# A decoder layer with 160 experts: a shared expert worked off at the end, and routing reordered

## The reference

```python
x = layernorm(x + self_attention(x))             # 16 heads of 16
x = layernorm(x + cross_attention(x, ctx_1024))  # similarity attention over the context
x = layernorm(x + experts(x))

# cross_attention: 16 sequences of 128, w1, w2, w3 = thirds of w_sim
Sim   = (hc @ w1)[:, :, None] + (hq @ w2)[:, None, :] + einsum('bid,bjd->bij', hc * w3, hq) + b
A     = softmax(Sim, axis=2)
hq_hat = A @ hq
Batt  = softmax(max(Sim, axis=2), axis=1)
hc_bar = sum_i Batt_i * hc_i
out   = concat([hc, hq_hat, hc * hq_hat, hc * hc_bar]) @ W_qv + b_qv

# experts: 160 of them, 8 for each token
probs = sigmoid(x @ router_w.T + expert_bias)
top_w, top_idx = top_k(probs, 8); top_w = 2.5 * top_w / sum(top_w)
routed = sum over the 8 of weight * (silu(x @ w_gate[e].T) @ w_down[e].T)
shared = silu(x @ w_gate_shared.T) @ w_down_shared.T
out = routed + shared
```

## Time and profile before

| | us | share of the span |
|---|---|---|
| median of 3 runs | 1225.49 | |
| the profiled execution | 1215.55 | |
| its span | 1213.7 | |
| TensorE matmul busy | 884.6 | 73% |
| TensorE weight load busy | 584.8 | 48% |
| VectorE busy | 542.4 | 45% |
| ScalarE busy | 437.9 | 36% |
| GpSimd busy | 394.1 | 32% |

### The profile page before, as it was taken

How to read it: one execution, slowest core, us unless ns; L and a number is a source line. 1 busy time by engine, 2 the same in 40 slices (tenths; PEclk the granted TensorE clock), 3 DMA queues, 4 the chain that set the end, 5 groups by cost and what they waited for, 6 DMA issues and landing times. The chain is left out here.

```text
span 1213.7 us, 17246 instructions
## 1 busy us (share of the span) xinstructions
PE 884.6 (73%) x4098; PEld 584.8 (48%) x4098; DVE 542.4 (45%) x1287; ACT 437.9 (36%) x942; POOL 394.1 (32%) x398
## 2 busy tenths in 40 slices
PE   8989999996697958677100578777787877786291
PEld 4433333432474735445100467666666656665271
DVE  1867777771327636465360122222232222222087
ACT  3257767775315142241000233333343433343011
POOL 7000000000000162543737255555555555555000
PEclk9979999998799978878655688898897888988596
DMA  7999999985101132221315677777777787774492
GB/s 251 296 371 334 326 365 360 347 307 174 45 35 53 50 111 97 76 84 53 126 67 206 213 229 241 232 227 222 232 235 244 220 235 224 227 232 114 188 420 82
DMA packets 113323, 247.22 MB, mean 204 GB/s; under 512 B 29378, under 2 KB 49770, under 8 KB 107008
## 3 DMA queue, kind: packets, MB, share of 16 engines
q1 hardware_dynamic: 92928, 209.39, 53.0%
q0 software_dynamic: 18240, 35.22, 8.0%
q10 hardware_dynamic: 2112, 2.10, 0.5%
HBM read 137.12 MB, written 125.70 MB: 217 GB/s over the span
## 5 line engine op out<-in xcount | busy, mean ns | idle before, releaser
L1517 POOL DMA_INDIRECT contributions<-e_y,e_dest x252 | 245.1, 973 | 227.5 <-ACT e_y L1504 158.6
L1483 DVE COPY e_xt<-e_psx 128x256 f32<-128x256 f32 (+1 forms) x196 | 97.1, 499 | 304.1 <-PE e_psx L1426 184.5
L1437 PE MATMUL e_psg<-e_xt,e_w 128*128 128x128 f32 (+1 forms) x784 | 173.7, 350 | 70.4 <-issue 35.9
L1648 POOL DMA_INDIRECT row_pool<-rows,places x128 | 125.6, 981 | 243.0 <-issue 159.1
L1446 PE MATMUL e_psy<-e_w,e_g 128*128 128x256 f32 x504 | 163.5, 429 | 40.9 <-ACT e_g L1497 21.1
L1437 PEld LDWEIGHTS e_psg<-e_xt,e_w 128*128 128x128 f32 x784 | 130.5, 219 | 86.9 <-issue 43.0
L493 DVE TENSOR_REDUCE a_mx<-a_psS 128x2 f32<-128x1024 f32 x128 | 152.2, 1218 | 35.5 <-PE a_psS L316 35.4
L451 ACT ACTIVATE a_e<-a_psT 128x512 f32<-128x512 f32 x256 | 137.8, 596 | 60.7 <-PE a_psT L346 52.8
L1504 ACT ACTIVATE e_y<-e_psy,e_weight 128x256 f32<-128x256 f32 x252 | 113.2, 473 | 98.7 <-PE e_psy L1446 55.6
L1497 ACT ACTIVATE e_g<-e_psg 128x128 f32<-128x128 f32 (+1 forms) x196 | 60.3, 308 | 197.6 <-PE e_psg L1437 119.6
L1426 PE MATMUL e_psx<-c_ident,e_x 128*128 128x128 f32 x504 | 96.1, 294 | 45.0 <-DMA e_x<-row_pool 44.9
(11 more groups left out here) (220 smaller groups left out, 981.1 us busy)
## 6 DMA issues: line engine op xcount, KB each, us to landing
row_pool<-fill SPq DMA_DIRECT2D x32, 1820.0 KB, 10.9
e_w<-w SPq DMA_DIRECT2D x196, 256.0 KB
e_x<-row_pool SPq DMA_DIRECT2D x140, 140.0 KB
c_c<-contributions SPq DMA_DIRECT2D x16, 1024.0 KB, 13.7
e_x<-row_pool SPq DMA_DIRECT2D x56, 280.0 KB
a_k<-k_parts SPq DMA_DIRECT2D x64, 128.0 KB, 5.8
a_q<-q_parts SPq DMA_DIRECT2D x32, 128.0 KB, 7.2
a_q<-q_parts SPq DMA_DIRECT2D x64, 64.0 KB, 6.9
```

The source lines that it names most:

```text
L1437: last = nc.tensor.matmul(psG[:, f.k % 2, 0:n], W[:, f.slot, c * INTER:(c + 1) * INTER], XT[:, f.k % 2, c * n:(c + 1) * n], start=c == 0, ...
L1483: nc.vector.tensor_copy(XT[:, at.k % 2, 0:n], psX[:, at.k % 2, 0:n]).then_inc(xt_done, 1)
L1517: nc.gpsimd.indirect_dma_start(out=contrib, out_offset=bass.IndirectOffsetOnAxis(ap=dest[:, page(f) + k:page(f) + k + 1], axis=0), in_=Y[: ...
L1648: nc.gpsimd.indirect_dma_start(out=pool, out_offset=bass.IndirectOffsetOnAxis(ap=place[:, b % 2, t, k:k + 1], axis=0), in_=rows[:, b % 2, ...
```

## The change

- The four similarities of a step go to banks 4, 5, 2 and 3 (`SIMILAR`), and none of them waits for an exponent. `rank` uses banks 0 to 2 and now waits for the third exponent.
- The numbers of the chosen experts come from an index search (`max_index`) in the choice, one for each tile, with a conversion of the result and the weights' product. `pack` and `unpack` are gone, with their buffers.
- `grow` moves from behind the products to ahead of the attention sums, `places` and the signal `rows_done` from behind the products to ahead of them.
- The shared expert leaves the steps. The last step has it for all four batches: gates 0 and 1 ahead of `rank`, gates 2 and 3 behind, four sigmoids on ScalarE, then, behind the tables, four gate multiplications, four products and four sums. The four results have buffers that the stage no longer needs by then, and SP stores all four behind its loads of the weights.
- Batch 2's scatters are in three groups: tile 0; tile 1 behind the end of mixing of batch 3; tiles 2 and 3 behind the router's products of batch 3.
- `rows`, `places` and `x2t` have four buffers, one for each batch, and the normalization no longer waits for scatters two batches back.

How the instructions stand is shown for four places. In these rows a name without a prefix is a tile in SBUF or memory, `m_ps` is the PSUM of the stage, and "x4" means four alike in a row.

The diff, cut to its core (the bodies of the removed functions are in the listing above):

```diff
+SIMILAR = (4, 5, 2, 3)
+GATES = (3, 6, 7, 5)
+SHARES = (0, 2, 6, 0)
...
-        X1T, ET, HQ, PR, X2T = (sb(f"m_{n}", [P, DC, S]) for n in ("x1t", "et", "hq", "pr", "x2t"))
-        GS, XS = sb("m_gs", [P, S]), sb("m_xs", [P, TT, D])
+        X1T, ET, HQ, PR = (sb(f"m_{n}", [P, DC, S]) for n in ("x1t", "et", "hq", "pr"))
+        X2T = sb("m_x2t", [P, B, DC, S])
         A, AT = sb("m_a", [P, TT, S]), sb("m_at", [P, TT, S])
+        GS, XS = A, (O, X1, X1b, AT[:, 0:2].rearrange("p a (t d) -> p (a t) d", d=D))
...
+        names8 = sb("m_names8", [P, TT, TOP_K], U32)
...
+                sp.dma_start(x2d[b], XS[b][:]).then_inc(x2_stored, 16)
...
-                store(n)
...
-            store(B - 2)
-            store(B - 1)
...
+            for b in range(B):
+                store(b)
...
-                    dispatch(b, sent[b % 2], range(TT))
+                    dispatch(b, sent[b % 2], (0,))
+                    pool_eng.wait_ge(mixed, TT * B)
+                    dispatch(b, sent[b % 2], (1,))
+                    pool_eng.wait_ge(routed, B)
+                    dispatch(b, sent[b % 2], (2, 3))
...
-                pe.wait_ge(shared_added, m_done)
...
+            def gate(b):
+                for c in range(DC):
+                    last = nc.tensor.matmul(ps[:, GATES[b]], Ws[:, c * INTER:(c + 1) * INTER], X2T[:, b, c],
...
+                last.then_inc(shared_gated, 1)
...
+                pe.wait_ge(shared_silu, b + 1)
+                if b == 3:
+                    pe.wait_ge(shared_added, 1)
+                out = two(SHARES[b])
...
+                    last = nc.tensor.matmul(out[:, t], GS[:, b, t * P:(t + 1) * P], Ws[:, DC * INTER:], start=True, stop=True)
...
                 if not part_b:
-                    share(n)
+                    gate(0)
+                    gate(1)
                     rank(n)
+                    gate(2)
+                    pe.wait_ge(lg_done, B)
+                    gate(3)
                     pe.wait_ge(spread_done, 1)
                     for i in range(3):
                         last = nc.tensor.matmul(ps[:, 4, i * P:(i + 1) * P], ones32[:], spread[:, i], start=True, stop=True)
                     last.then_inc(tables_spread, 1)
+                    pe.wait_ge(ranks_read, B)
+                    for b in range(B):
+                        share(b)
...
                 def similarity(i):
-                    if i >= 2:
-                        pe.wait_ge(row_expd, tile(i - 2))
...
-                        last = nc.tensor.matmul(ps[:, 4 + i % 2], ET[:, c, i * P:(i + 1) * P], CT[:, c],
+                        last = nc.tensor.matmul(ps[:, SIMILAR[i]], ET[:, c, i * P:(i + 1) * P], CT[:, c],
...
-                if part_c:
-                    share(n)
...
                 if part_c:
+                    pe.wait_ge(row_expd, tile(TT - 2))
                     rank(n)
...
-                for c in range(DC):
...
+                        nc.scalar.activation(A[:, i], ps[:, SIMILAR[i]], ACT.Exp, bias=nmax[:, i:i + 1],
...
+                    for b in range(B):
+                        act.wait_ge(shared_gated, b + 1)
+                        nc.scalar.activation(GS[:, b], ps[:, GATES[b]], ACT.Sigmoid).then_inc(shared_sigmoid, 1)
...
-                if n >= 2:
-                    act.wait_ge(sent[n % 2], n // 2 * (16 * TT * TOP_K))
...
+                normalize(nc, rows[:, n, :, 0:D], two(4), y[:, TT:], shift[:, TT:], normed2)
...
-                def gate_shared():
...
+                    for t in range(TT):
+                        do(nc.vector.max_index(names8[:, t], top[:, t], pr[:, t]))
+                    o2.hold()
+                    do(nc.vector.tensor_scalar(rows[:, n - 1, :, NAMES:ROW].bitcast(I32), names8[:], -1.0, float(EXPERTS),
+                                               ALU.mult, ALU.add))
+                    do(nc.vector.tensor_tensor(rows[:, n - 1, :, D:CODES], top[:], repeated(winv[:], 2, TOP_K), ALU.mult))
+                    sync()
+                def gate_shared(b):
...
+                def add_shared(b):
...
-                def pack():
...
-                def unpack():
...
-                    do(nc.vector.tensor_scalar(place[:, u_], k8[:], -1.0, FAR, ALU.mult, ALU.add))
-                    do(nc.vector.tensor_copy(rows[:, u_, :, CODES:NAMES], slots[:]))
...
                     dve.wait_ge(similar, tile(i))
-                    nc.vector.tensor_reduce(nmax[:, i:i + 1], ps[:, 4 + i % 2], AX, ALU.max, negate=True).then_inc(row_maxed, 1)
...
-                if part_c:
-                    gate_shared()
...
-                if part_c:
-                    pack()
-                    add_shared()
...
                 if part_c:
                     count_rows()
-                if part_c and not part_b:
-                    unpack()
                 if part_b:
                     dve.wait_ge(g_spread, n + 1)
                     nc.vector.tensor_scalar(ng[:], ps[:, 4, P:P + 1], -1.0, None, ALU.mult).then_inc(ng_done, 1)
-                if part_c and part_b:
-                    unpack()
+                if part_c:
+                    grow()
+                if part_c and not part_b:
+                    places()
+                    dve.sem_inc(rows_done, 1)
...
+                if part_c and part_b:
+                    places()
+                    dve.sem_inc(rows_done, 1)
...
-                if part_c:
-                    grow()
-                    places()
-                    dve.sem_inc(rows_done, 1)
...
                     dve.sem_inc(tables_done, 1)
+                    for b in range(B):
+                        gate_shared(b)
+                    for b in range(B):
+                        add_shared(b)
...
+        rows = ctx.enter_context(nc.sbuf_tensor("rows", [P, B, TT, ROW], F32))
...
+        place = ctx.enter_context(nc.sbuf_tensor("places", [P, B, TT, TOP_K], U32))
```

More of the change, by code:

```diff
@@ L565, in normalize @@
                              bias=shift[:, i:i + 1]).then_inc(done, 1)
-CONSTS = {"ident": P, "below": P, "far": EXPERTS, "home": EXPERTS, "expert": EXPERTS, "field": EXPERTS, "entry": 3, "slot": TOP_K * TT}
+CONSTS = {"ident": P, "below": P, "far": EXPERTS, "home": EXPERTS, "expert": EXPERTS, "entry": 3, "slot": TOP_K * TT}
 COL = {}
@@ L798, in rank, with share @@
                 last.then_inc(ranked, 1)
-            def share(m_done):
-                pe.wait_ge(shared_silu, m_done)
-                out = two(0)
+            def gate(b):
+                for c in range(DC):
+                    last = nc.tensor.matmul(ps[:, GATES[b]], Ws[:, c * INTER:(c + 1) * INTER], X2T[:, b, c],
+                                            start=c == 0, stop=c == DC - 1)
+                last.then_inc(shared_gated, 1)
+            def share(b):
+                pe.wait_ge(shared_silu, b + 1)
+                if b == 3:
+                    pe.wait_ge(shared_added, 1)
+                out = two(SHARES[b])
                 for t in range(TT):
-                    last = nc.tensor.matmul(out[:, t], GS[:, t * P:(t + 1) * P], Ws[:, DC * INTER:], start=True, stop=True)
+                    last = nc.tensor.matmul(out[:, t], GS[:, b, t * P:(t + 1) * P], Ws[:, DC * INTER:], start=True, stop=True)
                 last.then_inc(shared_made, 1)
@@ L906, in step @@
                     project_heads(n + 1)
[L907 removed]
+                turn(rows[:, n], 6, x2_turned, normed2, n * TT)
                 pe.wait_ge(x2t_done, n + 1)
@@ L912, in step @@
                     for c in range(DC):
-                        last = nc.tensor.matmul(lgs[:, t, 0:EXPERTS], X2T[:, c, t * P:(t + 1) * P], Wr[:, c],
+                        last = nc.tensor.matmul(lgs[:, t, 0:EXPERTS], X2T[:, n, c, t * P:(t + 1) * P], Wr[:, c],
                                                 start=c == 0, stop=c == DC - 1)
@@ L917, in step @@
                     turn_x1(n + 1)
-                for c in range(DC):
-                    last = nc.tensor.matmul(ps[:, 6], Ws[:, c * INTER:(c + 1) * INTER], X2T[:, c],
-                                            start=c == 0, stop=c == DC - 1)
-                last.then_inc(shared_gated, 1)
             run(pe, start, step)
@@ L1083, in add_shared @@
+                def add_shared(b):
+                    dve.wait_ge(shared_made, b + 1)
+                    shared = two(SHARES[b])
                     for t in range(0, TT, 2):
[L1084 removed]
+                        last = nc.vector.tensor_tensor(XS[b][:, t:t + 2], shared[:, t:t + 2], rows[:, b, t:t + 2, 0:D], ALU.add)
                     last.then_inc(shared_added, 1)
[L1087 to L1098 removed]
@@ L1173, in places @@
                     o2.hold()
-                    do(nc.vector.tensor_scalar(place[:, u_], k8[:], -1.0, FAR, ALU.mult, ALU.add))
-                    do(nc.vector.tensor_copy(rows[:, u_, :, CODES:NAMES], slots[:]))
+                    do(nc.vector.tensor_scalar(place[:, n - 1], k8[:], -1.0, FAR, ALU.mult, ALU.add))
```

(1 more changed line is left out.)

61 lines of the change are left out of this document (7 added, 54 removed).

## The result

The changed kernel takes 1192.55 us (median of 4 runs, 1191.65 to 1195.01) beside 1225.52 us of the kernel before: ratio 0.9734, 95% interval 0.9716 to 0.9751. The forecast was 1191. Its profiled execution took 1192.81 us, span 1190.8. The size came out; the way to it was another in part.

A forecast was written before the change was run, and what follows sets the result against it. GpSimd's scatters were taken to bound the end of mixing: 34.7 us earlier less 1 gives 34, so 1215.55 profiled becomes 1181.6, plus 9.9 for timed runs, 1191 us. The range was 1168 to 1209.

The forecast's parts named there:

- The bound: End of mixing: GpSimd's queue is the bound; batch 3's last scatter starts at 629.9 instead of 664.56, 34.7 us earlier.
- the 1 us for scatters beside VectorE's work: Last 48 back-to-back scatter issues: some slowed beside counts, tables and shared expert, 1 us taken, between 0 and 7.
- rival B: Similarities of steps 2 and 3: their signals are not held, starts near 433 and 493; gain 54 us, 1171; chance 0.22.
- The reference time: Whole kernel: profiled execution goes from 1215.55 to 1181.6 us; 9.9 added for the median of timed runs, 1191.
- All of it lies under the scatters: hidden: Shared expert between 590 and 631: loads to 613, stores by 620, no cost; without that cover some 20 us.
- Rival D: End of mixing: table's signal held until batch 3's scatters are out, stores open the barrier at about 675; 1229; chance 0.06.
- Gone is one gate product, off the path: Each mixing step: one gate product of TensorE leaves, off the path, so no time was counted for it.
- The index search: Choice ahead of row maximum 2: costs 1.8 us; with packing and shared sum moved away, gains 2.2 us per step.
- The counts fill the idle stretch: VectorE ahead of the attention sums: 9.9 us of counts fill idle time; only step 3 runs about 0.9 us late.
- The wait costs nothing: Batch 2's last sixteen scatters wait for the router's products: no cost while batch 3's places are not ready.
- The hold: Mixing stage: TensorE's signals are seen late in long unbroken scatter runs, some 2.3 to 4 us behind the last issue.
- A: The forecast itself: similarities of steps 2 and 3 both held, row maxima near 448 and 518; gain 34 us; chance 0.50.

The follow-up runs named there:

- r1: The kernel before, unchanged, profiled again in another surrounding: 1049.24 us.
- r9: The changed kernel with an unread gate product of TensorE put back in steps 0 to 2: 1039.57 us, ratio 0.9944 to the kernel before.
- r5: The changed kernel, unchanged, run again in another surrounding: 1040.79 us beside 1045.69 of the kernel before, ratio 0.9964.
- r7: The kernel before with the index search in place of packing and unpacking, nothing else: 1037.47 us, ratio 0.9939 to the kernel before.
- r3: The changed kernel with growing, places and the rows' signal behind the products again: 1040.82 us, ratio 0.9931 to the kernel before.
- r4: The changed kernel with batch 2's 32 scatters in one run again: 1036.44 us, ratio 0.9899 to the kernel before.

## Why the prediction was right, and where it was wrong

- **The bound** was right: the end of the mixing stage follows batch 3's first scatter. It followed batch 2's last with 0.3 us of idle, as forecast. The four index searches took 0.32 us each, and the 1 us for scatters beside VectorE's work came to 1.4 (62.0 us from 560.57 to 622.55, for 47 steps of 1.29).
- **Two errors cancelled.** The last scatter was forecast for 629.9 and started at 622.55, 7.4 us better, because the similarities were not held (434 and 498, near rival B's 433 and 493): row maximum 1 of step 3 came at 503.8, not at 519.0. Of these 15 us the rest of the step, with its 3.88 us of held signal and the early growing, gave 6.6 back. The barrier came 9.8 us worse than the forecast's distance from the last scatter. 34 forecast, 32.2 measured at the barrier. That these met is luck, not method.
- **The reference time** was luck too. The sum gave 1181.6 us for a profiled execution, and that took 1192.81. The forecast added 9.9 us, because the profiled execution of before was so much faster than its timed runs; the profiled execution of after was not, and its part behind the barrier is 9.3 us longer. r1 was to tell why, and could not, since it ran elsewhere; it stays open.
- **"All of it lies under the scatters: hidden"** failed. The 14 loads were sized at 11.6 us; in that surrounding 13 of them took 38.86. The shared products were not thought of as held at all; two of their sums waited 18.38 and 16.23 us, and the last store went out behind the last sum. Both paths ended within about 1 us of each other. Rival D had the stores as the opener of the barrier, by held tables; the tables were in time (587), the queue behind them was slow.
- **"Gone is one gate product, off the path"** failed in the first step: with it goes what kept TensorE's clock up, and row maximum 1 comes 1.5 us (r9 against r5) to 2.5 us (r7 against r3) later. In the later steps the clock fell with the product as well.
- **The index search** was right in price, 1.7 us (forecast 1.8), but worth 5.4 us in the step from 375, not 2.2, and 0.3 and 0.8 in the next two, which began at the lower clock in r7 and at the higher in r1. In the first the packing had also left TensorE idle: from 383 to 400 us it was busy for 11.6 of 17 us in r1 and for 13.5 in r7, at a granted clock of 0.71 and 0.90.
- **"The counts fill the idle stretch"** failed: the stretch was 6.91 us with 3.4 of unpacking beside it, but the faster row path shortened it to 6.01, and growing takes 9.9. It costs 2.4 to 2.8 us a step (r5 against r3) and brings batch 2's rows forward all the same.
- **"The wait costs nothing"** failed: the queue was the bound, and it paused for 2.30 and 2.88 us. Batch 3's places were ready at 579.2 and its first scatter went out at 581.54, so by an estimate from these rows up to 2.3 us of it was lost in the first result; where nothing is held it is some 3 to 4 us (r4). Whether the groups gained anything where signals were held was not tried.
- **The hold** was taken as given, in A as in B. The traces show that most of the gain comes from what it cost the kernel before, and that it comes and goes with the surrounding. No experiment was made with it there, so what sets it on stays open.

## What to carry to other kernels

A wait that no dependence explains may belong to the surrounding: profile the unchanged kernel again elsewhere before you price its removal. Where work leaves an engine, ask what its clock does in the gap, and where work fills an idle stretch, whether the other edits leave that stretch as long. A queue that is the bound is not to be given pauses. And where two late paths end together, the removal of one gains little.

## What the runs showed of the hardware

In the surrounding of the first result, SP took 38.86 us for 13 loads beside GpSimd's scatters, and VectorE stood idle up to 18.38 us for products that had ended; in the other, with the same code, the 14 loads took 8.55 us and this wait was 0.44 (r5). Of the 149 us between the two spans, 15 lie ahead of the barrier and some 133 behind it. The expert stage, where GpSimd scatters too, has such waits as well. VectorE's copies behind TensorE, the changed kernel in the first result and then r5:

```profile
L1464 DVE COPY e_xt<-e_psx 128x256 f32<-128x256 f32 (+1 forms) x196 | 97.2, 500 | 275.5 <-PE e_psx L1407 148.6
```

```profile
L1464 DVE COPY e_xt<-e_psx 128x256 f32<-128x256 f32 (+1 forms) x196 | 96.3, 500 | 175.1 <-PE e_psx L1407 165.0
```

One copy takes the same 500 ns; the idle time before them is 100 us longer, and 74.8 us of it, in 27 waits, are put down to "remote", none in r5.
